# First attention layer: queries and keys projected from one flat band instead of four overlapping windows

## The reference

```python
x = x + _L0_conv_ref(_gn(x), w_qkv, b_qkv)     # windowed attention: changed
x = x + _L1_conv_ref(_gn(x), ...)              # untouched, like the two after it

def _L0_conv_ref(x, w_qkv, b_qkv):             # x: 4 images, 256 channels, 64 x 64
    qkv = einsum('nchw,dc->ndhw', x, w_qkv) + b_qkv
    # 8 heads of 32 channels; each pixel attends to the 5 x 5 pixels around it
    scores = einsum('ngdhw,ngdhwk->nghwk', qh, k_win)
    scores = where(inside the image, scores, -inf)
    att = softmax(scores)
    out = einsum('nghwk,ngdhwk->ngdhw', att, v_win)
```

## Time and profile before

| | |
|---|---|
| median of 3 runs | 7823.7 us |
| the profiled execution: its time, its span | 7822.81 us, 7821.0 us |
| first attention layer, steady part of the span | about 100 to 1283 us |
| PE busy over the whole span | 93% |
| DVE, POOL, ACT busy over the whole span | 72%, 60%, 47% |

### The profile page before, as it was taken

How to read it: one execution, slowest core, us unless ns; L and a number is a source line. 1 busy time by engine, 2 the same in 40 slices (tenths; PEclk the granted TensorE clock), 3 DMA queues, 4 the chain that set the end, 5 groups by cost and what they waited for, 6 DMA issues and landing times. The chain is left out here.

```text
span 7821.0 us, 136128 instructions
## 1 busy us (share of the span) xinstructions
PE 7267.6 (93%) x52034; PEld 6191.0 (79%) x52034; DVE 5658.2 (72%) x8853; ACT 3661.9 (47%) x7040; POOL 4728.1 (60%) x2194
## 2 busy tenths in 40 slices
PE   5999998989998999599999999999999999996999
PEld 4777776879998777378888788888888887886999
DVE  5666665334443455589999999999999999996664
ACT  3655565423332333155555555555555555554222
POOL 3555553023333000189999899999999898995332
PEclk9999998999999999799999999999999999998999
DMA  3111112865555975133323333333333233324452
GB/s 145 63 59 59 61 68 81 292 177 146 145 145 154 264 198 156 54 66 82 78 66 72 77 80 70 74 76 69 76 85 74 64 75 78 81 57 127 148 162 78
DMA packets 660646, 818.18 MB, mean 105 GB/s; under 512 B 468598, under 2 KB 501494, under 8 KB 630247
## 3 DMA queue, kind: packets, MB, share of 16 engines
q1 hardware_dynamic: 581318, 483.44, 22.1%
q0 software_dynamic: 61504, 298.03, 16.1%
q10 hardware_dynamic: 17376, 30.54, 1.1%
HBM read 397.01 MB, written 193.76 MB: 76 GB/s over the span
## 5 line engine op out<-in xcount | busy, mean ns | idle before, releaser
L1963 POOL TENSOR_TENSOR e_ev<-e_se,e_v 128x1536 f32<-128x1536 f32 (+1 forms) x832 | 3107.9, 3936 | 162.8 <-ACT e_se L1896 162.5
L2064 DVE SCALAR_TENSOR_TENSOR e_stage<-e_k,e_rl,e_qp 128x512 f32<-128x512 f32 x3136 | 2231.6, 746 | 251.1 <-ACT e_se L1896 196.5
L1896 ACT ACTIVATE e_se<-e_stage 128x512 f32<-128x512 f32 x2880 | 1708.4, 597 | 1488.7 <-PE e_stage L1707 1416.5
L1714 PE MATMUL e_pv_sum<-e_ident,e_ev 128*128 128x128 f32 x12544 | 1790.5, 273 | 4.6 <-POOL e_ev L1963 4.4
L1707 PE MATMUL e_stage<-e_top,e_minus 128*128 128x512 f32 x3136 | 1585.5, 506 | 118.1 <-DVE e_stage L2064 108.8
L1714 PEld LDWEIGHTS e_pv_sum<-e_ident,e_ev 128*128 128x128 f32 x12544 | 1479.4, 141 | 153.8 <-issue 92.6
L1714 PE MATMUL e_pe_sum<-e_ident,e_se 128*128 128x128 f32 x8448 | 1271.3, 273 | 41.3 <-ACT e_se L1896 41.3
L1714 PEld LDWEIGHTS e_pe_sum<-e_ident,e_se 128*128 128x128 f32 x8448 | 1051.8, 140 | 226.9 <-ACT e_se L1896 54.0
L911 POOL DMA_DIRECT2D agg<-c_ot x384 | 334.7, 874 | 882.0 <-ACT c_ot L989 772.4
L403 POOL TENSOR_TENSOR a_pr<-a_pr,a_rden 128x480 f32<-128x480 f32 x512 | 494.6, 987 | 544.4 <-DVE a_rden L636 544.4
L1707 PEld LDWEIGHTS e_stage<-e_top,e_minus 128*128 128x128 f32 x3136 | 596.7, 190 | 285.0 <-DVE e_stage L2064 203.8
(11 more groups left out here) (180 smaller groups left out, 12479.1 us busy)
## 6 DMA issues: line engine op xcount, KB each, us to landing
e_acc<-e_se POOLq DMA_DIRECT2D x192, 1024.0 KB, 7.3
qkv<-b_ot SPq DMA_DIRECT2D x120, 512.0 KB, 5.9
c_xt<-qkv SPq DMA_DIRECT2D x384, 160.0 KB, 3.8
agg<-c_ot POOLq DMA_DIRECT2D x384, 160.0 KB, 2.5
f_ws<-in_L_w_sets SPq DMA_DIRECT2D x32, 1152.0 KB, 7.8
a_xb<-in_x SPq DMA_DIRECT2D x24, 768.0 KB, 5.1
a_xr<-in_x SPq DMA_DIRECT2D x32, 512.0 KB, 3.8
x<-a_xr SPq DMA_DIRECT2D x32, 512.0 KB, 2.8
```

Of the source, the lines that this page charges most:

```text
L1714: last = nc.tensor.matmul(total[:, c * PART:(c + 1) * PART], lhsT=src[:, c * PART:(c + 1) * PART], rhs=ident[:], is_transpose=True, start= ...
L1896: nc.scalar.activation(exps(t, j), stage[:, bank_of(t, j), :], ACT.Exp).then_inc(exp_done, 1)
L1963: nc.gpsimd.tensor_tensor(split(ev[(t * NG2 + g) % NEV][:, 0:size]), split(exps(t, o * K2 + i, size)), window(v[h], h, u, o, i, size), ALU ...
L2064: nc.vector.scalar_tensor_tensor(rows(stage[:, bank_of(t, j), :]), win, rl[:, h, o:o + 1], rows(qp[:]), ALU.add, ALU.mult).then_inc(multip ...
```

## The change

`x_high`, `x_low` and `kb` become flat: 776 elements (`FLAT`), laid out as `xb` is. Keys are projected from the flat band in two contiguous parts of 386 (`KPART`) for each half of the output channels, the queries from its 512 contiguous inner elements. The windows as before are kept for the values alone, in new tiles `v_high` and `v_low`. Thus ACT and POOL each do a flat pass besides the windowed one, for each half of the channels. `scores` reads the keys of a tile through `window`: 12 runs of 20 elements, 64 apart, starting at element 2 + 16c. The query copy sorts the columns into tiles as it goes.

```diff
+        EDGE = GUARD - K0 // 2
+        FLAT = BROWS * WW + 2 * GUARD
+        KPART = BROWS * WW // 2 + K0 // 2
-        x_high = [sb(f"x_high{u}", [PART, HALVES, TILES, NK], F32R) for u in range(2)]
+        x_high = [sb(f"x_high{u}", [PART, HALVES, FLAT], F32R) for u in range(2)]
+        v_high = [sb(f"v_high{u}", [PART, HALVES, TILES, NK], F32R) for u in range(2)]
...
+        def window(x, c, first=0, rows=KR):
+            a = x[:, EDGE + first * WW + c * TC:EDGE + first * WW + c * TC + 1]
+            return bass.AP(tensor=a.tensor, offset=a.offset, ap=[a.ap[0], [WW, rows], [1, KC]])
...
-                last = nc.gpsimd.tensor_tensor(tiled(x_low[u % 2], h), areas(xb[u % 2], h),
-                                               tiled(x_high[u % 2], h).bitcast(F32), ALU.subtract)
+                nc.gpsimd.tensor_tensor(x_low[u % 2][:, h], xb[u % 2][:, h], x_high[u % 2][:, h].bitcast(F32), ALU.subtract)
+                last = nc.gpsimd.tensor_tensor(tiled(v_low[u % 2], h), areas(xb[u % 2], h),
+                                               tiled(v_high[u % 2], h).bitcast(F32), ALU.subtract)
...
-                            rhs = tiled(x[u % 2], h)[:, :, K0 // 2:K0 // 2 + TR, K0 // 2:K0 // 2 + TC]
+                            first, size = GUARD + K0 // 2 * WW, BAND0
                         else:
-                            rhs = x[u % 2][:, h, c * PAIR:(c + 1) * PAIR, :]
+                            first, size = EDGE + c * KPART, KPART
+                        rhs = x[u % 2][:, h, first:first + size]
...
-                        for w, x in ((w_high, x_high), (w_high, x_low), (w_low, x_high)):
+                        for w, x in ((w_high, v_high), (w_high, v_low), (w_low, v_high)):
...
-                                                rhs=kb[u][rows[i], e, c, :], start=False, stop=True, skip_group_check=True)
+                                                lhsT=qb[u][rows[i], e, c, :], rhs=window(kb[u][rows[i], e], c),
...
-                nc.scalar.activation(tiled(x_high[u % 2], h), areas(xb[u % 2], h), ACT.Copy).then_inc(x_high_ready, 1)
+                nc.scalar.activation(x_high[u % 2][:, h], xb[u % 2][:, h], ACT.Copy)
+                nc.scalar.activation(tiled(v_high[u % 2], h), areas(xb[u % 2], h), ACT.Copy).then_inc(x_high_ready, 1)
...
-                    nc.scalar.activation(qb[u % 2][:, m].rearrange("p c q -> p (c q)"), pj[:, 0:BAND0],
+                    nc.scalar.activation(qb[u % 2][:, m].rearrange("p c (r x) -> p r c x", x=TC),
+                                         pj[:, 0:BAND0].rearrange("p (r c x) -> p r c x", c=TILES, x=TC),
```

More of the change, by code:

```diff
@@ L222, in window_attention @@
         mr = [sb(f"mr{u}", [PART, TILES, NK], F32R) for u in range(2)]
-        x_high = [sb(f"x_high{u}", [PART, HALVES, TILES, NK], F32R) for u in range(2)]
-        x_low = [sb(f"x_low{u}", [PART, HALVES, TILES, NK], F32R) for u in range(2)]
+        x_high = [sb(f"x_high{u}", [PART, HALVES, FLAT], F32R) for u in range(2)]
+        x_low = [sb(f"x_low{u}", [PART, HALVES, FLAT], F32R) for u in range(2)]
+        v_high = [sb(f"v_high{u}", [PART, HALVES, TILES, NK], F32R) for u in range(2)]
+        v_low = [sb(f"v_low{u}", [PART, HALVES, TILES, NK], F32R) for u in range(2)]
         qb = [sb(f"qb{u}", [PART, HALVES, TILES, TQ]) for u in range(2)]
-        kb = [sb(f"kb{u}", [PART, HALVES, TILES, NK]) for u in range(2)]
+        kb = [sb(f"kb{u}", [PART, HALVES, FLAT]) for u in range(2)]
         vt = [sb(f"vt{u}", [KCH, 2, C]) for u in range(NV)]
@@ L279, in window_attention @@
         MEASURE_AT = 3
+        def window(x, c, first=0, rows=KR):
+            a = x[:, EDGE + first * WW + c * TC:EDGE + first * WW + c * TC + 1]
+            return bass.AP(tensor=a.tensor, offset=a.offset, ap=[a.ap[0], [WW, rows], [1, KC]])
         def areas(x, h):
-            a = x[:, h, GUARD - K0 // 2:GUARD - K0 // 2 + 1]
+            a = x[:, h, EDGE:EDGE + 1]
             return bass.AP(tensor=a.tensor, offset=a.offset, ap=[a.ap[0], [TC, TILES], [WW, BROWS], [1, KC]])
@@ L438, in project @@
                         if what == 0:
-                            rhs = tiled(x[u % 2], h)[:, :, K0 // 2:K0 // 2 + TR, K0 // 2:K0 // 2 + TC]
-                            out = pj[:, 0:BAND0].rearrange("p (c r x) -> p c r x", c=TILES, x=TC)
-                        else:
-                            rhs = x[u % 2][:, h, c * PAIR:(c + 1) * PAIR, :]
-                            out = pj[:, 0:PAIR * NK].rearrange("p (c k) -> p c k", k=NK)
-                        last = nc.tensor.matmul(out, lhsT=w[:, h, what * C + m * PART:what * C + (m + 1) * PART], rhs=rhs,
+                            first, size = GUARD + K0 // 2 * WW, BAND0
+                        else:
+                            first, size = EDGE + c * KPART, KPART
+                        rhs = x[u % 2][:, h, first:first + size]
+                        last = nc.tensor.matmul(pj[:, 0:size], lhsT=w[:, h, what * C + m * PART:what * C + (m + 1) * PART], rhs=rhs,
                                                 start=k == 1, stop=k == 2 * 3)
@@ L483, in scores @@
                     for i in range(2):
-                        last = nc.tensor.matmul(ps[:, 2 * s + i, e * NK:(e + 1) * NK], lhsT=qb[u][rows[i], e, c, :],
-                                                rhs=kb[u][rows[i], e, c, :], start=False, stop=True, skip_group_check=True)
+                        last = nc.tensor.matmul(ps[:, 2 * s + i, e * NK:(e + 1) * NK].rearrange("p (r x) -> p r x", x=KC),
+                                                lhsT=qb[u][rows[i], e, c, :], rhs=window(kb[u][rows[i], e], c),
+                                                start=False, stop=True, skip_group_check=True)
                 last.then_inc(scored, 1)
@@ L581, in copy_qk @@
                 if what == 0:
-                    nc.scalar.activation(qb[u % 2][:, m].rearrange("p c q -> p (c q)"), pj[:, 0:BAND0],
+                    nc.scalar.activation(qb[u % 2][:, m].rearrange("p c (r x) -> p r c x", x=TC),
+                                         pj[:, 0:BAND0].rearrange("p (r c x) -> p r c x", c=TILES, x=TC),
                                          ACT.Identity, bias=bias[:, m:m + 1]).then_inc(qk_copied, 1)
                 else:
-                    to = kb[u % 2][:, m, c * PAIR:(c + 1) * PAIR, :].rearrange("p c k -> p (c k)")
-                    nc.scalar.activation(to, pj[:, 0:PAIR * NK], ACT.Identity,
+                    first = EDGE + c * KPART
+                    nc.scalar.activation(kb[u % 2][:, m, first:first + KPART], pj[:, 0:KPART], ACT.Identity,
                                          bias=bias[:, HALVES + m:HALVES + m + 1]).then_inc(qk_copied, 1)
```

## The result

The changed kernel has a median of 7871.76 us over 4 runs (7868.7 to 7881.1). The kernel before, run beside it, has 7822.84 us over 4 runs (7819.49 to 7824.48). The ratio is 1.0061, with an interval from 1.0048 to 1.0073: 49 us or 0.6% slower. My 7834 us are 38 us too low, and the time lies above my range. Of the runs further down, one execution of e4 took 21375 us at a mean granted clock of 0.33; its ratio leaves that one out.

The account below looks back on a forecast made before the run. The prediction took PE, busy 1180.81 of 1183 us, to bound the first layer. Its terms, -55.2 + 15.4 + 48.6 + 0.9 = +9.7 us, gave 7834 us, 0.13% more; range 7812 to 7861.

Parts of the forecast that it names:

- shorter projections: Key and query matmuls on PE: narrower or contiguous columns save 1.78 us a band, 55.2 us over 31 bands.
- windowed key reads: Q by k product in scores: reading 12 runs of 20 adds 0.48 us a band, 15.4 us over 32 bands.
- waits for POOL: PE waits 1.62 us for POOL's late weights, once a band, 30 times: 48.6 us added.
- before the loop: Ahead of the first projection: two flat POOL passes add 3.06 us, ACT's 0.2, shorter projections give back; net +0.9 us.
- POOL's flat pass, added: In split on POOL: a contiguous subtraction of 776 elements per channel half, 1.53 us each, 3.06 us a band.
- My bounds of 1.44 and 1.73: Limits for POOL's flat pass: 1.44 us by the masks, 1.73 us by the weights' subtraction.
- rival (c): POOL's contiguous subtraction costs 1.73 us: 12 us more, 7846 us; chance 0.17.
- The stall: In step 0's turn of the weights, PE would wait 1.62 us for its second head, one stall a band.
- The key reads: Broken runs in scores: taken at 15 ns per 12 runs, with bounds of nothing and 40 ns a pair.
- ACT's pass: ACT's added flat rounding, at most 1.03 us after steps 6 and 7: no cost, perhaps a few tenths at step 0's start.

Follow-up runs that it names:

- e4: Changed kernel with POOL's windowed subtraction for the values moved to steps 3 and 4 of the following band, with its own signal: 7773.79 us, ratio 0.9934.
- e3: Changed kernel with scores reading 240 contiguous key elements instead of the window, hence other keys: 7872.95 us, ratio 1.0061.
- e5: Changed kernel with POOL's flat pass cut from 776 to 640 elements after the first two bands: 7838.39 us, ratio 1.0018.
- e12: Changed kernel with x_high and x_low kept 2 elements (8 bytes) further on in their tiles: 7831.52 us, ratio 1.0012.
- e6: Changed kernel with x_low_ready signalled after the second flat pass, the windowed pass having its own semaphore: 7894.59 us, ratio 1.0102.
- e9: Changed kernel with POOL trial subtractions of windowed and packed shapes put first: 960 elements, windows from element 2 against a packed input, 1.90 us; both packed 2.21.
- e7: Changed kernel with 26 POOL subtractions put ahead of the first layer to time shapes: contiguous 960 took 2.22 us, 776 from one tile 1.48.
- e11: Changed kernel with POOL trial subtractions, second input shifted by 32 to 1024 elements, output shifted, windows from element 0: 776 stayed at 1.82 to 1.83 us.
- e10: Changed kernel with two plain fp32 matmuls of 400 columns put on PE in step 2's wait: 7869.27 us, ratio 1.0057.
- e2: Kernel before the change with both flat passes, on ACT and POOL, added into tiles that nothing reads: 7931.95 us, ratio 1.0138.
- e8: Changed kernel with 12 short fp32r matmuls of 256 columns put on PE in step 2's wait: 7941.8 us, ratio 1.015.

## Why the prediction was wrong

**What the first layer's 45 us are made of**, by the steps of the prediction, in us:

| step | predicted | measured | how |
|---|---|---|---|
| shorter projections | -55.2 | -49 | 31 x 1.58, from steps 3 to 6 and one more 0.24 |
| windowed key reads | +15.4 | 0 | e3 |
| waits for POOL | +48.6 | +73 | 30 x (1.96 + 0.24 + 0.23), steps 2 and 1 |
| clock | none | +16 | 13 x 1.26 |
| before the loop | +0.9 | +3.9 | first `scores` at 104.72 for 100.79 |
| sum | +9.7 | +44 | the layer's end: +45.2 |

**The step that failed: "POOL's flat pass, added", at 1.53 us.** I scaled the mean of four pieces, and took it for the nearest since it is the same kind of instruction at a like size. Two of the four are windowed splits: they read 960 elements in windows that begin 8 bytes away from the packed input, which is the cheap case. The other two are `normalise`, whose second input is one value repeated over each row. The flat pass reads both inputs from the same element. It costs 1.83 us. My bounds of 1.44 and 1.73 didn't hold it: the masks read one tile twice, and the weights' 3428 ns for 1536 elements I scaled without its fixed part, though that was the one row with two inputs, both contiguous. 0.2 us and 2.1 ns an element make 3.4 of it, and 1.83 of 776. Two passes of 0.30 us more, 30 times, are 18 us; e5 shows what the kernel does at my price, e12 that the price hangs on the offset. My rival (c) named this side, up to 1.73; that end was too low as well.

The Trainium skill, "GPSIMD Engine Reference", section 3.1, with its 2.6 cycles an element, gave an estimate of 1.68 us for the pass. That is nearer than my value, and the measurement is still above it.

**The stall: place wrong, chain right.** I let PE wait in step 0's turn. It waits one part earlier, in `project` at `at` = 2, for the `x_low_ready` of the split just done; I had not asked whether the band that is projected there is the one just split. It is the same chain, so this moved the wait rather than doubling it, as e6 shows. My 1.62 us a band, with 0.60 for the longer passes and 0.18 for key reads that are free (PE arrives 0.24 earlier, POOL's chain starts 0.06 earlier), make 2.40. Measured are 2.20 at step 2, and at step 1, which I had called nearly a stall and counted as none, 0.23: 2.43.

**The clock, missing from the sum.** The earlier trace rows show 1.00 over a stretch in which PE never stood still. That says nothing about a kernel that stands still once a band. I had reckoned a wait at its own length. The falls cost a further 16 us; at waits of 1.44 us (43.1 / 30 in e5) for 1.80 (53.9 / 30) they are 3 in place of 13, so the price of the pass brought some 13 us this way too, beside the 18 of its own length.

**The key reads: the upper and the middle value wrong, the lower bound right.** I carried the fp32r price of a broken run over to plain fp32, by a difference of 10 ns between a merged row and an estimated end. e3 shows nothing there. Alone this would have made me some 10 us too high (15.4, less 5.4 by which an earlier PE waits longer); it hid as much of the errors above, by luck. Beside this, my sum comes to 7833.4 us, and I wrote 7834.

**The projections** gain 1.58 us a band for 1.78. A key part gains 0.24 us where 0.27 was expected, the two query parts 0.63 for 0.70; keys stand 0.177 us apart and queries 0.232, for 0.175 and 0.229, which is a part of it. The rest was not traced. **ACT's pass** cost nothing, as said: exponentials of step 0 wait 0.23 us for DVE after it, so its cover was nearly used up. **Before the loop** two flat passes of 1.8 us, for 1.53, delay the first projection from 78.67 to 82.60 us; what is gained by narrower keys is lost again, since the clock rises later (about 105 us for 96) and more of the first parts runs at the lower level.

## What to carry to other kernels

A pass added to an engine that is 55% busy must be placed where that engine has a gap; taken out of the one unbroken chain of the band and done five steps later, a pass of the same length left the kernel 98 us faster (e4 against the changed kernel). Look whether two pieces of work under one signal are needed at the same time: here only the flat half was urgent, and moving the other turned 0.6% slower into 0.7% faster. And price a new pass by a row that is alike in the number of inputs, the layout and the starts of the operands, not in the size alone.

## What the runs showed of the hardware

- A POOL subtraction of two tiles takes about 0.2 us and 2.1 ns an element when both inputs begin at the same offset (776: 1.82 us; 960: 2.22), and 1.56 for 776 (e12) and 1.90 for 960 (e9) when one begins 2 elements (8 bytes) further. Shifts by 4, 8 and 32 to 1024 elements don't help, and neither does moving the output alone by 8 or 256 elements (e7, e11). Offsets of 1 and 3 elements weren't measured.
- One wait of 1.8 us in each band of 38 us, with PE busy otherwise, let the granted clock fall to the lower level 13 times in 30 bands, for 3.4 us each (one 6.8). With the wait filled it never fell (e10); with a wait of 1.4 us it fell 3 times (e5) and twice (e12). The wait's length does not settle it: with 1.8 us in a longer band it fell in 29 bands of 30 (e2), and with the wait one part later, in pieces of 1.5 and 0.3 us, in 21 (e6). That stays unexplained.
- In the plain fp32 matmuls of `scores`, a moving operand of 12 runs of 20 elements costs no more than a contiguous one (e3). In fp32r broken runs did cost: 0.287 us for 512 columns in runs of 16, 0.232 contiguous in the changed kernel; 0.183 for 0.173 us when 6 runs of 64 were shifted by one element.
- Twenty-four more instructions a band on PE brought waits on issue of up to 5.5 us (e8). What runs short there is open.
